# Score tiles as two one-slot units, and masked maxima of one head over two key chunks

## The reference

```python
energy = jnp.einsum('nqhd,nkhd->nhqk', q, k)
energy = jnp.where(mask == 0, jnp.float32(-1e+20), energy)
attn = jax.nn.softmax(energy / math.sqrt(EMBED), axis=3)
out = jnp.einsum('nhql,nlhd->nqhd', attn, v).reshape(N, q_len, HEADS * HEAD_DIM)
```

## Time and profile before

| | kernel before |
|---|---|
| median of 3 runs | 3425.52 us (3421.22 to 3428.02) |
| profiled execution | 3398.36 us, its span 3396.6 us |
| mean granted clock of TensorE | 0.971 |
| PE busy | 3242.2 us (95% of the span) |
| DVE busy | 1980.8 us (58%), 4289 instructions |
| ACT busy | 1446.3 us (43%) |
| POOL busy | 955.0 us (28%) |
| wide attention and block 2 | about 0 to 1850 us |
| experts of block 2 | about 1850 to 2040 us |
| blocks 3 and 4, from the first `max3` | 2043 us to the end |

### The profile page before, as it was taken

How to read it: one execution, slowest core, us unless ns; L and a number is a source line. 1 busy time by engine, 2 the same in 40 slices (tenths; PEclk the granted TensorE clock), 3 DMA queues, 4 the chain that set the end, 5 groups by cost and what they waited for, 6 DMA issues and landing times.

```text
span 3396.6 us, 71446 instructions
## 1 busy us (share of the span) xinstructions
PE 3242.2 (95%) x30986; PEld 1431.6 (42%) x31007; DVE 1980.8 (58%) x4289; ACT 1446.3 (43%) x1645; POOL 955.0 (28%) x469
## 2 busy tenths in 40 slices
PE   7999999999999999999997979899999999999999
PEld 3444444444434444444433753223333334343344
DVE  4444456554655546565575028677777777766446
ACT  3444344445434453344433212355454454545533
POOL 4655554654465445555400000100000000000000
PEclk9999999999999999999988999899999999999989
DMA  4000000000000000000021622565343444443300
GB/s 152 12 13 13 28 12 15 7 11 33 7 21 12 13 28 7 21 12 12 4 116 39 188 81 75 132 175 158 97 120 115 127 124 117 118 118 113 115 26 20
DMA packets 85306, 221.17 MB, mean 65 GB/s; under 512 B 18424, under 2 KB 39168, under 8 KB 84224
## 3 DMA queue, kind: packets, MB, share of 16 engines
q1 hardware_dynamic: 79616, 201.65, 19.5%
q0 software_dynamic: 5376, 14.95, 2.0%
HBM read 204.61 MB, written 18.48 MB: 66 GB/s over the span
## 4 chain that ended last, share of the span: by engine, by line
PE 84%; DVE 6%; ACT 4%; POOL 3%; issue 1%; DMA 1%; ACTq 0%; POOLq 0%; DVEq 0%
PE ring L1294 13%; PE pv L1179 10%; PE ring L1168 9%; PE pv L1310 9%; PE ring L1246 3%; PE ring L1149 3%; PE ring L1140 3%; PE ring L1126 3%; PE ring L1141 3%; PE ring L1165 3%; PE ring L1127 2%; PE ring L1290 2%; POOL wide L1554 2%; PE ring L1367 2%; PE ring L1348 2%; PE ring L1260 2%
## 5 line engine op out<-in xcount | busy, mean ns | idle before, releaser
L1554 POOL TENSOR_TENSOR wide<-wide 124x1024 f32<-124x1024 f32 (+1 forms) x341 | 803.9, 2358 | 180.2 <-ACT wide L1450 142.2
L1457 ACT ACTIVATE wide<-ring 128x1024 f32<-128x1024 f32 (+1 forms) x544 | 536.2, 1023 | 498.4 <-PE ring L1294 494.6
L1671 DVE TENSOR_REDUCE max_a<-ring 128x2 f32<-128x802 f32 x512 | 493.4, 991 | 395.9 <-PE ring L1149 395.5
L1450 ACT ACTIVATE wide<-ring 124x1024 f32<-124x1024 f32 (+1 forms) x416 | 425.3, 1026 | 438.1 <-PE ring L1168 385.0
L1294 PE MATMUL ring<-slim 32*32 32x512 f32 (+1 forms) x7040 | 522.9, 607 | 0.3 <-DVE slim L1724 0.2
L1699 DVE CUSTOM_DVE_ANT_0 rest<-ring,slim 128x401 bf16<-128x401 f32 x683 | 374.9, 576 | 106.0 <-PE ring L1246 71.1
L1168 PE MATMUL ring<-wide 64*124 64x512 f32 (+1 forms) x1664 | 424.7, 588 | 0.0
L1179 PE MATMUL pv<-wide 124*64 124x512 f32 (+1 forms) x1664 | 413.9, 613 | 8.2 <-ACT wide L1450 8.2
L1709 DVE TENSOR_REDUCE slim<-ring 128x2 f32<-128x1024 f32 x256 | 308.0, 1222 | 111.9 <-PE ring L1260 105.4
L1524 POOL DMA_DIRECT2D slim<-in_ctx_k x16 | 8.9, 558 | 968.5 <-PE ring L1246 920.2
L1551 POOL TENSOR_TENSOR wide<-wide 124x1024 f32<-124x1024 f32 x31 | 73.1, 2357 | 599.5 <-ACT wide L1450 586.2
(11 more groups left out here) (238 smaller groups left out, 3964.3 us busy)
## 6 DMA issues: line engine op xcount, KB each, us to landing
slim<-masks SPq DMA_DIRECT2D x832, 128.0 KB, 2.7
slim<-in_ctx_k SPq DMA_DIRECT2D x16, 800.5 KB, 4.6
wide<-in_w_pair SPq DMA_DIRECT2D x32, 384.0 KB, 3.0
wide<-in_w SPq DMA_DIRECT2D x16, 512.0 KB, 4.7
wide<-in_we SPq DMA_DIRECT2D x16, 512.0 KB, 3.7
slim<-in_ctx_v SPq DMA_DIRECT2D x16, 442.0 KB, 5.9
wide<-in_ctxT SPq DMA_DIRECT2D x4, 1601.0 KB, 6.8
slim<-in_ctx_k POOLq DMA_DIRECT2D x16, 400.2 KB, 4.8
```

The source lines that it names most:

```text
L1450: sc.activation(exps_a[0:kn, slot_of[unit], :], slot[0:kn, :], ACT.Exp, scale=WIDE ** -0.5).then_inc(scalar_done, 1)
L1457: sc.activation((exps_2 if blk == 2 else exps_34)[0:kn, first + 2 * i:first + 2 * i + 2, :].rearrange("p h n -> p (h n)"), ring_t[0:kn, ba ...
L1554: po.tensor_tensor(sums[0:kn, :], sums[0:kn, :], view, ALU.add).then_inc(pool_done, 1)
L1671: ve.reduce_max(max_a[:, :, q, c], slot.rearrange("p (h n) -> p h n", h=2)[:, :, 0:CHUNK], AX.X).then_inc(vector_done, 1)
```

## The change

- `max3` changes its shape. A unit is now one query tile, **one head** and **two key chunks** (`c` in 0, 1), so there are still 32 units for each group, at the same places of the order. TensorE still issues 8 matmuls, four query strips for each of two chunks, but all eight lie on the strip of one head: four tiles, each used twice. The unit still fills both banks of one slot. DVE issues one instruction over 2 x 401 columns in place of two of 401.
- `maskQ` is laid out on the host by chunks, 4 x 401 columns instead of 1601, so that two chunks lie side by side. It takes 12 more elements on each partition. `max_b` holds two maxima of each head and query tile instead of four. The third scratch row for DVE is moved and all three are 802 long; tiles behind the mask move by four columns.
- `scoreb` becomes two units, one for each pair of heads, each with one slot. The strings of turns have the digits of these streams doubled in place (6 to 66 in `TURNS_1`, 1 to 11 and 5 to 55 in `TURNS_3`), so the order of the other units is kept, and TensorE and ACT issue the same instructions of the score tiles with the same kinds of waits.
- The planner's model is changed: it knows four row strips of the array, which step uses which (`rows`), and other durations for these steps. So it may pick other slots and other counts of dummy matmuls.

```diff
     def slim_maxima(blk, b, g):
         if blk == 3:
             for q in range(QT):
-                for c in range(len(CTX_CHUNKS)):
-                    for hp in range(2):
-                        yield Step(0.17 if b or g else 0.8, (("ve", 1.12),), 1, (("low", b, g),), ("max3", b, g, q, hp, c),
-                                   (16, 16 if b or g else 1))
-                        unit = emit(in_slot(("max3", b, g, q, hp, c), "vector"))
+                for c in range(len(CTX_CHUNKS) // 2):
+                    for h in range(GROUP):
+                        yield Step(0.36 if b or g else 0.8, (("ve", 0.96),), 1, (("low", b, g),), ("max3", b, g, q, h, c),
+                                   (16, 16 if b or g else 1), rows=(h,) if b or g else range(4))
+                        unit = emit(in_slot(("max3", b, g, q, h, c), "vector"))
...
-            unit = ("scoreb", blk, b, g, k)
...
-            in_slots(unit, "scalar_first", "scalar")
-            i = expo.take()
-            plan.slot[unit], plan.slot_free[unit] = i, expo.free[i]
-            emit(unit)
+            place = expo.take()
+            for half in range(2):
+                unit = ("scoreb", blk, b, g, k, half)
+                yield Step(lasts, (("sc", 1.02),), 1, (("rowb", blk, b, g),) + ((("pvb", blk, *behind),) if behind else ()), unit,
+                           divided, rows=(2 * half, 2 * half + 1))
+                plan.slot[unit], plan.slot_free[unit] = place, expo.free[place]
+                emit(in_slot(unit, "scalar"))
...
                 elif kind == "max3":
-                    b, g, q, hp, c = a
+                    b, g, q, h, c = a
                     past.wait_ge(*at("dma", "load_low", b, g))
                     past.wait_ge(*at("vector", "low", b, g))
+                    own = slice(PAD * h, PAD * (h + 1))
                     for i, j in product(range(2), range(P // PAD)):
-                        own = slice(PAD * (2 * hp + i), PAD * (2 * hp + i + 1))
+                        c0 = CTX_CHUNKS[2 * c + i]
                         last = pe.matmul(slot[j * PAD:(j + 1) * PAD, i * BANK:i * BANK + CHUNK],
                                          queries_low(3, g)[own, q * P + j * PAD:q * P + (j + 1) * PAD],
-                                         keys_low(3, g)[own, CTX_CHUNKS[c]:CTX_CHUNKS[c] + CHUNK], start=True, stop=True)
+                                         keys_low(3, g)[own, c0:c0 + CHUNK], start=True, stop=True)
...
-                    for i in range(2):
-                        after(junk_free[0])
-                        ve.tensor_tensor_reduce(out=max_junk[junk], in0=slot[:, i * BANK:i * BANK + CHUNK],
-                                                in1=maskQ_sb[:, q, CTX_CHUNKS[c]:CTX_CHUNKS[c] + CHUNK],
-                                                scale=1.0, scalar=-3e38, op0=ALU.add, op1=ALU.max,
-                                                accum_out=max_b[:, 2 * hp + i, q, c:c + 1]).then_inc(vector_done, 1)
-                        junk, junk_free = (junk + 1) % 3, junk_free[1:] + [n + i + 1]
+                    after(junk_free[0])
+                    ve.tensor_tensor_reduce(out=max_junk[junk].rearrange("p (i n) -> p i n", i=2),
+                                            in0=slot.rearrange("p (i n) -> p i n", i=2)[:, :, 0:CHUNK],
+                                            in1=maskQ_sb[:, q, 2 * c * CHUNK:2 * (c + 1) * CHUNK].rearrange("p (i n) -> p i n", i=2),
+                                            scale=1.0, scalar=-3e38, op0=ALU.add, op1=ALU.max,
+                                            accum_out=max_b[:, h, q, c:c + 1]).then_inc(vector_done, 1)
+                    junk, junk_free = (junk + 1) % 3, junk_free[1:] + [n + 1]
```

More of the change, by code:

```diff
@@ L98, in lay_out @@
     ctx_k[:, :, STRIP] = ctx.reshape(B, CTX, GROUPS, GROUP * SLIM).transpose(0, 2, 3, 1)
+    maskQ = np.stack([mask[:, c0:c0 + CHUNK] for c0 in CTX_CHUNKS], 1).reshape(S, -1)
     maskT = np.zeros((NKT * P, S), np.int32)
@@ L180, with __init__ @@
+    "74744447445555464554645546444674455554645546455464446744555546455446455464474765575565565576676"
 )
 class Step:
-    def __init__(self, pe=0.0, use=(), slots=0, needs=(), name=None, parts=(1, 1), first=None, second=0.0, mark=None, late=0.0):
+    def __init__(self, pe=0.0, use=(), slots=0, needs=(), name=None, parts=(1, 1), mark=None, late=0.0, rows=range(4)):
         self.pe, self.use, self.slots, self.needs, self.name = pe, use, slots, needs, name
-        self.parts, self.first, self.second, self.mark, self.late = parts, first, second, mark, late
+        self.parts, self.mark, self.late, self.rows = parts, mark, late, tuple(rows)
@@ L194 @@
 class Pace:
     def __init__(self):
[L198 removed]
+        self.pe, self.parts, self.issued = 0.0, 1, 0.0
+        self.busy = [0.0] * 4
         self.lane = {"ve": 0.0, "sc": 0.0, "po": 0.0}
@@ L201, in __init__, with idle_until @@
         self.done, self.picked, self.spare = {}, [], None
+    def idle_until(self, time):
+        self.pe = max(self.pe, time)
+        self.issued, self.busy = self.pe, [self.pe] * 4
     def accept(self, step):
@@ L209, in accept @@
         if step.pe:
[L210 to L217, removed]
+            at = max(at, self.issued)
+            if step.parts[0] != self.parts:
+                free = max(self.busy) + DIVIDE
+            else:
+                free = max(self.busy[r] for r in step.rows)
+            if self.spare and at - max(self.busy) >= WARM_FROM:
+                self.spare(at - max(self.busy))
+            self.issued = at + ISSUE
+            end = max(at, free) + step.pe
+            for r in range(4):
+                self.busy[r] = end if r in step.rows else max(self.busy[r], end - step.pe) if step.parts[0] != self.parts else self.busy[r]
+            self.pe, self.parts = max(self.busy), step.parts[1]
         last, marked = end, end
         for i, (lane, time) in enumerate(step.use):
[L220 to L225, removed]
+            ready = end + HOP if i == 0 else last if lane == step.use[i - 1][0] else last + HOP
             last = self.lane[lane] = max(self.lane[lane], ready) + time
@@ L342, in in_slot @@
         slot_free[i] = ((lane, unit),)
[L343 to L348, removed]
         return unit
@@ L1108, in _ @@
                         past.wait_ge(*at(lane, *other))
-                    slot = slot_tile(unit) if kind != "scoreb" else None
+                    slot = slot_tile(unit)
                 if kind == "turn":
@@ L1399, in _ @@
                 n = plan.begin["scalar", unit]
-                slot = slot_tile(unit) if unit in bank_of and kind != "scoreb" else None
+                slot = slot_tile(unit) if unit in bank_of else None
                 if kind == "setup":
```

146 lines of the change are left out of this document (67 added, 79 removed).

## The result

The changed kernel took 3459.3 us, the median of 4 runs (3457.0 to 3463.9). The kernel before took 3426.8 us beside it (4 runs). The ratio of the runs is 1.010, with a 95% interval of 1.0082 to 1.0117: 1.0% slower, +32.5 us. The forecast was +30 us, 3455 us.

A forecast was written before the change was run, and what follows sets the result against it. TensorE in order was taken as the bound, with the three slots close behind. Opening 5.4, later followers 27 and slots -2 sum to +30 us: 3455 us on the median, 0.9% slower; range 3398 to 3495 us.

The forecast's parts named there:

- Part 1: VectorE's maximum: one instruction of 802 for two of 401 saves 0.08 us per unit, 41 us of VectorE over 512.
- Part 2: TensorE's max3: using four tiles twice adds 0.17 us to a unit; +5.4 us in the opening, +27 us after it.
- 5.4 + 27 = 32 us: Second round's cost: 5.4 us for 32 opening units, 27 us passed on from followers of the whole array and score tiles.
- 58% of 39 us: Share passed on of the 39 us for 228 max3 with a unit of the whole array next.
- the discount of 42%: Share of block 3's score halves, 176 of 416, that wait for a slot anyway, so TensorE's lateness loses less.
- Part 3: Slot turns with a max3: freed 0.09 us later if taken up at once, 0.08 earlier if queued; -2 us.
- Part 4: Score tiles as two units: only the planner's slot picks and dummies can differ; 0, with 10 us to either side.
- A: Score halves behind maxima queued at VectorE: slots decide and the kernel gets faster, 3405 us; chance 0.25.
- the 47 us: Second round's cost before discount: 39 us for units of the whole array, 8 us for score tiles behind a max3.
- B: Maxima before 32x32 units or overlapping score halves: second round hides behind other tiles, +3 us, 3429 us; chance 0.15.
- C: Everywhere: TensorE sets the pace, all lateness passed on and slots freed late, +74 us, 3500 us; chance 0.13.
- The 3384 us: Time if VectorE were the bound and its 41 us of saved work all counted; the forecast did not adopt it.

The follow-up runs named there:

- The last run: Changed kernel with only the 228 max3 units that have a unit of the whole array next put back on two heads' strips; 3434.3 us, ratio 1.0016.
- VectorE's part alone: Kernel before, its TensorE tiles and planner kept, but VectorE takes both heads of a unit in one instruction of 2 x 401; 3394.0 us, ratio 0.9993.
- the old kernel with the new picks: Kernel before with the slot picks of the changed kernel, nothing else different; 3413.6 us against 3397.7, ratio 1.0041.
- the two-strip kernel: Changed kernel with each unit's second chunk on the neighbouring head's strip, so eight tiles are used once; 3418.8 us against 3426.4, ratio 0.998.
- TensorE's part alone: Changed kernel, but VectorE takes the two chunks in two instructions of 401 columns, as before; 3450.8 us against 3397.7, ratio 1.0148.

## Why the prediction held

The mechanism was right: TensorE's second round makes the kernel slower by more than VectorE's instruction saves. At like clock the loss is 27 us where the forecast had 30. But the time also holds a term that the forecast did not have, a lower granted clock, about 13 us. That the first comparison came out at +32.5 us and not nearer to the 40 of the means of the later chip is luck of the forecast.

**Part 1, VectorE's instruction: right in size.** 991 ns where the row of the reduction was taken, 37 us less busy. (The upper bound of the gain adds up to 0.12 us, 82 ns and 0.04, not 0.13.)

**Part 2, the second round: mechanism and size right.** The gap to `pvb` is 0.45 us (forecast 0.46), the fills of the opening 1.21 us apart (1.21), so 32 x 0.16 = 5 us there. For the opening and the rest together the forecast had 5.4 + 27 = 32 us; undoing the round gives 35 us at like clock. As timed it is 46 us, and the 11 us between them are the clock's. How the 27 us were split is less certain. The forecast had 58% of 39 us, 23 us, for followers of the whole array and 5 us for the score tiles. The last run gives 19 and 11 us at like clock, 34 and 7 as timed. By the first reading the discount of 42% was about right in the sum, and by the second it was too large, 34 of 39 us being passed on. The maxima with another maximum behind them were put at 0, and no run takes them by themselves.

**Part 3, the slots: VectorE's saving was put too high.** Taken alone, without any second round, the forecast's row makes it 244 x 0.08 = 20 us. By the ratios the runs seem to disagree, with 2 us for VectorE's part alone and 21 us between the old kernel with the new picks (1.0041) and the two-strip kernel (0.998). At like clock they agree: 7 us for VectorE's part alone, 11 us between TensorE's part alone and the changed kernel, and 10 us between the two kernels with the new picks. So the saving is worth 7 to 11 us, a sixth to a quarter of VectorE's 41.

**Part 4, the picks: 0 forecast.** The forecast had thought of some ten picks; 903 of the 2888 differ, all of them in blocks 3 and 4. At like clock they cost 2 us in the old kernel and nothing in the new one. The 14 us of the old kernel are a lower clock, so other picks can cost what the clock makes of them, and that they summed to little here was luck.

**The term that was missing: the granted clock.** The forecast took the clock as unchanged in blocks 3 and 4. The changed kernel spends 31 us more at the lower level than the kernel before on the same chip, about 13 us of time. In its profile the clock from 2500 to 2800 us is 0.96, where it was 0.99.

At like clock it adds up so: the second round 35 us, less about 8 that VectorE's instruction saves, is the 27 us in the table. The clock's 13 us make it 40 by the means of that chip; the first comparison had 32.5.

**The rivals.** A (slots decide, faster) needed under a quarter of the 47 us to be passed on; at like clock 29 were. B (hidden behind other tiles) is seen in part: the 252 other units pay 0.03 to 0.04 us of their 0.17. C (all passed on) is not borne out at like clock; as timed it is near for the followers of the whole array. The 3384 us that the forecast set beside its own rest on the Trainium skill's advice ("TensorEngine Tiling (Array Packing)", PSUM Bottleneck), which speaks of tiles in the same bank; the change merges reads of two banks, and that alone gave 7 us at like clock.

## What to carry to other kernels

A unit that is packed into tiles held up the next one here until the second use of its tiles was over: the follower on the whole array started 0.45 us after it instead of 0.29, and 512 such units cost 35 us at like clock. So spread a unit over tiles that are not yet in use, and merge instructions on the reading engine only if that leaves the spread alone. Work taken off an engine that the chain hardly visits (here 41 us of VectorE at 2.0%) is worth a fraction at best; look at what the merge asks of the engine that the chain runs along. And before a difference of 1% is explained by waits, set the granted clocks of the two kernels side by side: here a shift of 0.001 in its mean goes with almost 3 us, and 14 us that looked like the price of other slots were the clock.

## What the hardware showed beside that

- Matmuls overtake each other across tiles. In the changed kernel (TensorE's timeline) the first round of a `max3` starts at 2110.72, the eight mask matmuls of the next unit at 2110.74 to 2110.77, and only then, at 2110.90, the four matmuls of the second round, which stand ahead of the masks in the program. 55 of the 92 score tiles behind a `max3` start so.

```profile
2110.72 0.35 PE L1244 MATMUL ring<-slim 32*32 32x401 bf16 x4
2110.74 0.41 PE L1283 MATMUL ring<-slim,ident_b 32*32 32x512 bf16 x8
2110.90 0.34 PE L1244 MATMUL ring<-slim 32*32 32x401 bf16 x4
```

  The Trainium skill ("TensorE: Matmul & The Clock Gate"), in "Step-by-step: what each phase is for", says that only weight loads are pulled ahead and matmuls stay in program order. This trace differs, and the measurement decides. It may also be why a second round in front of a 32x32 unit costs little (0.03 to 0.04 us); no run tests that alone.

- In two of the profiled executions, one with two dummies and one with three, the granted clock stood at 0.50, the 1.2 GHz level, in the opening group: in the first from 2039 to 2104 us, in the second from 2040 to 2077 us. TensorE was busy 57.8 us of the 58 from 2046 to 2104 us, and the fills took 1.76 us in the first instead of the expected 0.99. From 2035 to 2046 us TensorE had been busy for 5.3 us at a granted 0.69; but the changed kernel's profile has the same two numbers there, and its opening ran at 1.00. So that stretch does not tell what decides.
- The same binary has medians near 3398 us on two chips and near 3427 us on two others, 0.8% apart. That is nearly as much as the change under study. Some 16 of these 29 us go with the clock (190 and 193 us at the lower level against 229 and 233); where the others come from is open.
